# A sparse graph layer on one NeuronCore: the diagonal found among the candidates instead of in the full row, and the last tiles' order written anew

## The chip, the core and the metric

The kernel runs on one core of a Trainium2 chip. The metric is the time of the whole program on the device in microseconds, the median of several executions. Engines are named as in the profile: PE is TensorE, PEld its weight loads, DVE is VectorE, ACT is ScalarE, POOL is GpSimd, SP is SyncE, which only issues transfers.

## The reference

x is 8192x512 and adj is 8192x8192, both float32. adj is zero but for some nine entries a row (73,960 in all in the inputs that are drawn), the diagonal always among them, since it is `bernoulli(0.000488)` made symmetric, with the unit matrix added, times a uniform value between 0.05 and 5.42.

```python
h = max(layernorm(x), 0)
mask = adj > 0
head = mask / max(sqrt(sum(mask * mask, axis=-1)), 1e-12)
inc = adj + head
out = x + (inc @ h) / sum(inc, axis=-1)
```

So every row of the result is x plus a weighted mean of the few rows of h that its nonzero entries name.

## The kernel before

**Stages.** In the first 80 us the layer norm reads x, and h = relu(layernorm(x)) is written to a scratch tensor in DRAM. Then adj is read once, in 64 tiles of 128 rows. A tile is 128 x 8192 float32, 4 MB; it comes in four chunks of 1 MB, and a chunk j holds columns 1024j to 1024j+1023 of the left half and of the right half (runs of 4 KB). There are two tile buffers (`A`), so tile t+2 is loaded chunk by chunk into the buffer that tile t leaves (`load_chunk`, on SP's queue). A chunk may be overwritten when DVE has folded it and when ACT has run its two tests over the pair of chunks (`checked`).

**One tile on DVE.** For the first 61 tiles (`FOLDED`) DVE folds the two halves of a chunk into one word a column, right times 2^100 plus left (`fold`), takes the eight largest words (`find_values`) and their places (`find_places`). That is three passes of 1024 columns for each chunk, twelve a tile. Between them stand the small operations of the tile before, p = t-1, on 32 candidates a row (8 from each of 4 chunks): `tell_halves`, `low_words`, `values`, `counts` (which signs are set, and how many), `ranks` (the place of each spilled entry), `columns_any`, `columns`, `own_columns`, `heads`, `incs`, `inverse`, `weights`; and those of tiles t-2 and t-3 (`pay_places`; `find_entry`, `take_entry`, `sum_entry`). The two best candidates of every chunk are the row's own slots (8), the other 24 can spill: what is set among them is packed for the 128 rows together into 3 x 128 places by matmuls (`offsets`, `find_owner`, `bring_spill`). The last three tiles (61 to 63, "wide") are searched without folding, in eight parts of 1024 columns, and after them comes a batch tile (number 64, `BATCH`, here also called z) that does those rows again which the folded way could not do; its row numbers are found by `count_bad`, `pay_bad`, `pick_bad` and `list_rows` while the wide tiles run, and its adj rows come by one indirect transfer.

**The diagonal.** Of each folded tile the diagonal entry is treated apart. `read_diagonal` takes a strided 128x128 block of the chunk, multiplies it with the unit matrix and sums it to one value a row; `cut_diagonal` sets the diagonal's word in `F` to zero, so that it is no candidate; `keep_diagonal` copies the value to the front of the candidates. Its row of h is not gathered but computed again from x by ACT (`row_again`) and added by a matmul (in `residual`).

**The others.** POOL gathers rows of h from DRAM: 8 indirect transfers for the own slots (`gather_own`), 3 or 4 for the spilled ones (`gather_spill`); empty slots have a column beyond the tensor and are skipped. ACT builds the diagonal weight matrices (`own_matrices`), the spill matrix (`spill_matrix`), the root of the count (`roots`), the places (`reach_places`), and runs the tests (`check`, four a tile). PE multiplies: x by the unit matrix and the row again (`residual`), 8 own slots (`product_own`), 3 or 4 spill groups (`product_spill`). ACT copies the sum out (`finish_tile`), SP stores it.

**What sets the order.** Each engine's program is written out by hand: `period(t)` for tile t on ACT, DVE and PE, `wide_period` and `batch_period` on DVE, and `drain` for what is left when the last tile has been searched. Within `period(t)` p = t-1, q = t-2, r = t-3 and f = t-4. Nothing is scheduled otherwise. In the drains and in the batch period z, y, w and v are tiles 64, 63, 62 and 61.

## Time and profile before

| | |
|---|---|
| median of 3 runs | 1268.82 us (1267.47 to 1271.12) |
| the profiled execution, its own time | 1271.85 us |
| its span from first to last instruction | 1270.1 us |
| busy: PE, DVE, ACT, POOL | 78%, 94%, 77%, 60% |
| transfers | 471.00 MB, mean 371 GB/s |
| mean granted clock of TensorE | 0.905 |

The engines' shares say how busy each was over the span; the DMA share of a stretch is the mean over the core's 16 transfer engines. The span has three parts: the layer norm (to about 80 us), the loop over the folded tiles (to 1127 us), and the wide tiles with the batch tile and the drain (to 1270 us).

### The profile page before, as it was taken

To read this page: it belongs to the slowest core of one execution; us is meant where nothing else is said; L and a number is where in the kernel's file an instruction comes from. 1 tells how busy PE (TensorE), PEld (TensorE's weight loads), DVE (VectorE), ACT (ScalarE), POOL (GpSimd) and SP (SyncE) were. 2 spreads that over 40 slices of the span, in tenths; PEclk is the share of its full clock that TensorE was granted. 3 is DMA by queue.
4 is the path that set the end of the run, shared out by engine and by line. 5 is a ranking of instruction groups with operands and counts; after the bars stand their busy time and mean duration, and the time that the engine had idled before them with its cause. 6 is when DMAs were issued, how large, how long until landed. Compare 5 with 4: busy or idle time off the path is not lost.

```text
span 1270.1 us, 14707 instructions
## 1 busy us (share of the span) xinstructions
PE 987.8 (78%) x2682; PEld 483.4 (38%) x2682; DVE 1189.0 (94%) x2868; ACT 979.2 (77%) x1902; POOL 765.8 (60%) x748
## 2 busy tenths in 40 slices
PE   0003888988898899888889879888978898777677
PEld 0001444444444344444444334433433444443343
DVE  6679999999999999999999999999999999999971
ACT  6657788888888888888888888787887888884741
POOL 1003666666666676667666666667666677665562
PEclk9999899888889988888998998889888898888888
DMA  8999999999999999999999999999999999997542
GB/s 353 427 423 406 398 392 381 393 388 390 388 391 401 398 399 394 400 400 398 399 401 391 396 394 387 390 395 400 400 385 381 395 386 387 397 399 259 175 118 77
DMA packets 148208, 471.00 MB, mean 371 GB/s; under 512 B 24826, under 2 KB 24826, under 8 KB 143965
## 3 DMA queue, kind: packets, MB, share of 16 engines
q1 hardware_dynamic: 90368, 331.38, 66.4%
q0 software_dynamic: 57744, 138.64, 30.0%
q8 instruction: 25, 0.41, 0.1%
q14 instruction: 71, 0.58, 0.1%
HBM read 490.47 MB, written 33.82 MB: 413 GB/s over the span
## 4 chain that ended last, share of the span: by engine, by line
DVE 47%; DMA 25%; issue 14%; ACT 5%; SPq 4%; PE 4%; POOL 0%; DVEq 0%; another core or an unknown queue 0%; ACTq 0%; POOLq 0%
DMA adj_tile<-in_adj_dram 22%; DVE cand_word L797 14%; DVE folded L775 14%; DVE cand_index L801 5%; DMA gathered_rows<-in_x_dram 3%; DVE cand_index L820 2%; DVE cand_word L815 2%; PE acc L1330 2%; SPq L392 2%; ACT adj_tile L563 2%; ACT junk L576 1%; SPq L399 1%; PE acc L1341 1%; DVE diagonal_alone L782 1%; DVE entry L964 1%
## 5 line engine op out<-in xcount | busy, mean ns | idle before, releaser
L497 POOL DMA_INDIRECT gathered_rows<-h_scratch,slot_column x520 | 552.4, 1062 | 263.9 <-issue 158.6
L576 ACT ACTIVATE junk<-adj_tile,zero_unit 128x2048 bf16<-128x2048 f32 x256 | 510.4, 1997 | 89.8 <-issue 45.9
L1330 PE MATMUL acc<-gathered_rows,diag 128*128 128x512 f32 x1040 | 517.9, 655 | 2.4 <-DMA gathered_rows<-h_scratch,slot_column 1.9
L497 POOL DMA_INDIRECT gathered_rows<-h_scratch,spill_column x198 | 205.3, 1037 | 212.9 <-ACT spill_column L622 157.8
L1330 PEld LDWEIGHTS acc<-gathered_rows,diag 128*128 128x128 f32 x1040 | 216.9, 215 | 259.7 <-issue 258.9
L775 DVE SCALAR_TENSOR_TENSOR folded<-adj_tile 128x1024 f32<-128x1024 f32 x244 | 296.6, 1216 | 10.0 <-DMA adj_tile<-in_adj_dram 8.7
L797 DVE MAX8 cand_word<-folded 128x8 f32<-128x1024 f32 x244 | 298.7, 1224 | 3.6 <-issue 0.3
L801 DVE FIND_INDEX8 cand_index<-cand_word,folded 128x8 uint32<-128x1024 f32 x244 | 297.6, 1220 | 0.0
L1341 PE MATMUL acc<-gathered_rows,spill_matrix 128*128 128x512 f32 x396 | 182.4, 597 | 16.1 <-DMA gathered_rows<-h_scratch,spill_column 13.0
L639 ACT ACTIVATE diag<-ident,weights_and_payload 128x128 f32<-128x128 f32 x581 | 176.4, 388 | 21.9 <-DVE weights_and_payload L917 17.7
L1279 PE MATMUL poff<-spill_rank,lanes_before 128*128 128x1 f32 x130 | 24.1, 255 | 157.5 <-DVE spill_rank L862 156.3
L1341 PEld LDWEIGHTS acc<-gathered_rows,spill_matrix 128*128 128x128 f32 x396 | 72.0, 190 | 108.2 <-issue 108.1
L1324 PE MATMUL acc<-own_row,diag 128*128 128x512 f32 x122 | 76.7, 715 | 46.1 <-ACT own_row L649 20.4
L1279 PEld LDWEIGHTS poff<-spill_rank,lanes_before 128*128 128x128 f32 x130 | 24.9, 217 | 207.5 <-issue 123.0
L1302 PE MATMUL pbrought<-weights_and_payload,owner 128*128 128x72 f32 (+1 forms) x384 | 69.6, 328 | 17.2 <-DVE weights_and_payload L922 16.5
L1308 PE MATMUL pturned<-ident,owner 128*128 128x128 f32 x396 | 80.2, 356 | 2.2
L1308 PEld LDWEIGHTS pturned<-ident,owner 128*128 128x128 f32 x396 | 68.2, 253 | 6.6 <-ACT spill_matrix L630 6.0
L1319 PE MATMUL acc<-x_residual,ident 128*128 128x512 f32 x96 | 53.0, 636 | 19.9 <-issue 11.1
L1302 PEld LDWEIGHTS pbrought<-weights_and_payload,owner 128*128 128x128 f32 x384 | 60.4, 232 | 18.4 <-issue 18.3
L630 ACT ACTIVATE spill_matrix<-pturned,entry 128x128 f32<-128x128 f32 x198 | 56.8, 357 | 0.8 <-PE acc L1341 0.8
L1324 PEld LDWEIGHTS acc<-own_row,diag 128*128 128x128 f32 x122 | 21.4, 211 | 93.2 <-issue 58.8
L622 ACT ACTIVATE spill_column<-entry 128x3 uint32<-128x3 f32 (+1 forms) x65 | 13.0, 199 | 52.3 <-DVE entry L964 51.3
(151 smaller groups left out, 892.8 us busy)
## 6 DMA issues: line engine op xcount, KB each, us to landing
adj_tile<-in_adj_dram SPq DMA_DIRECT2D x256, 1024.0 KB
h_scratch<-adj_tile SPq DMA_DIRECT2D x16, 1024.0 KB, 10.5
out_dram<-out_tile SPq DMA_DIRECT2D x64, 256.0 KB
gathered_rows<-in_x_dram SPq DMA_DIRECT2D x12, 1024.0 KB, 12.6
x_residual<-in_x_dram SPq DMA_DIRECT2D x48, 256.0 KB
gathered_rows<-h_scratch,slot_column POOLq DMA_INDIRECT x520
x_held<-in_x_dram SPq DMA_DIRECT2D x4, 1024.0 KB, 7.9
gathered_rows<-h_scratch,spill_column POOLq DMA_INDIRECT x198, 3.5
```

The lines of the kernel that those rows point to most:

```text
L497: nc.gpsimd.indirect_dma_start(out=into, out_offset=None, in_=h[:, :], in_offset=bass.IndirectOffsetOnAxis(ap=column, axis=0), bounds_chec ...
L576: nc.scalar.activation(junk[:, n % 2].rearrange("p (j c) -> p j c", j=2), both[:, :, half], ACT.Relu, bias=zero_unit[:], scale=-UP, accum_ ...
L630: last = nc.scalar.activation(W[:, t % 2, g], pturned[:, g * P:(g + 1) * P], ACT.Copy, scale=entry[:, t % 2, g, 0:1])
L639: last = nc.scalar.activation(diag[:, t % 2, s], ident[:], ACT.Copy, scale=wpay[:, t % 2, s:s + 1])
L775: nc.vector.scalar_tensor_tensor(out=F[:, j % 2], in0=a[:, 1], scalar=UP, in1=a[:, 0], op0=ALU.mult, op1=ALU.add).then_inc(folded, 1)
L797: nc.vector.max(out=cv[:, t % 2, 8 * j:8 * j + 8], in_=F[:, j % 2]).then_inc(vals_found, 1)
L801: nc.vector.max_index(out=ci[:, t % 2, 8 * j:8 * j + 8], in_max=cv[:, t % 2, 8 * j:8 * j + 8], in_values=F[:, j % 2]).then_inc(idx_found, 1)
L1302: last = nc.tensor.matmul(bank[:, c:c + 3 * n], owner[:, g * P:(g + 1) * P], wpay[:, t % 2, 1 + OWN:1 + OWN + 3 * n], start=True, stop=True)
L1308: last = nc.tensor.matmul(pturned[:, g * P:(g + 1) * P], owner[:, g * P:(g + 1) * P], ident[:], start=True, stop=True)
L1324: nc.tensor.matmul(acc[t % 3][:], diag[:, t % 2, 0], again[:], start=False, stop=False)
L1330: last = nc.tensor.matmul(acc[t % 3][:], diag[:, t % 2, 1 + s], slot(t % 2, s), start=False, stop=False)
L1341: last = nc.tensor.matmul(acc[t % 3][:], W[:, t % 2, g], slot(t % 2, OWN + g), start=False, stop=(g == groups(t) - 1))
```

## The change

The loads stay as they are (runs of 4 KB). Three things change.

First, on DVE the three operations on the diagonal go (`read_diagonal`, `cut_diagonal`, `keep_diagonal`). The diagonal's word stays in `F` and so becomes a candidate like any other. After the search of tile p a new `find_diagonal(p)` compares the eight column numbers of the chunk that holds the diagonal with the row's own number (a new constant `diag_at`), multiplies with the eight values and sums them into the front of the candidates; `leave_diagonal(p)` subtracts what was found, so that the candidate counts as unset. `columns_any` comes earlier for this, `counts` and `ranks` later. The load no longer waits for `diag_read`. Three steps of `count_bad` on the diagonal go as well.

Second, on ACT `row_again(t)` waits for `row_added` (the matmul that read the row of tile t-1) instead of `own_done` (all own products of tile t-1), and `roots` comes behind `spill_matrix`.

Third, the orders of DVE, ACT, PE and POOL are written anew from tile 61 on.

```diff
             def fold(t, j):
...
-                if j == diag_chunk(t):
-                    read_diagonal(t)
-                    cut_diagonal(t)
...
+            def find_diagonal(t):
+                dve.wait_ge(cola_ready, t + 1)
+                dve.wait_ge(val_ready, t + 1)
+                nc.vector.scalar_tensor_tensor(out=own_entry[:], in0=in_diag_chunk(cola, t), scalar=diag_column(t),
+                                               in1=in_diag_chunk(val[:, 1:], t), op0=ALU.is_equal, op1=ALU.mult,
+                                               accum_out=val[:, 0:1]).then_inc(diag_found, 1)
+
+            def leave_diagonal(t):
+                dve.wait_ge(diag_found, t + 1)
+                rest = in_diag_chunk(val[:, 1:], t)
+                nc.vector.tensor_tensor(rest, rest, own_entry[:], ALU.subtract).then_inc(diag_left, 1)
...
             def row_again(t):
                 if t >= 1:
-                    act.wait_ge(own_done, t)
+                    act.wait_ge(row_added, t)
...
             # ACT, period(t)
                     if not wide(q):
                         row_again(q)
-                if small:
-                    roots(p)
                 if pay:
                     copy_owner(q)
...
                     spill_columns(r)
                     spill_matrix(r)
+                if small:
+                    roots(p)
...
             # DVE
             def wide_period(t):
                 p, q, r = t - 1, t - 2, t - 3
                 part_values(t, 0)
+                if p == FOLDED:
+                    no_diagonal()
+                pay_places(q)
                 tell_halves(p)
...
                 part_values(t, 4)
-                pay_places(q)
...
             def batch_period():
...
                 part_values(z, 0)
-                find_entry(v)
+                pay_places(w)
                 tell_halves(y)
                 low_words(y)
-                take_entry(v)
...
                 part_places(z, 3)
-                pay_places(w)
...
             # POOL
                 gather_spill(t - 2)
-                gather_own(t)
+                if t < BATCH:
+                    gather_own(t)
             gather_spill(BATCH - 1)
+            gather_own(BATCH)
             gather_spill(BATCH)
```

**DVE, one folded tile.** These rows of before are the start of the program of tile 34, from its first fold, where the diagonal lies in the first chunk (lines are those of the kernel before; L782 is `read_diagonal`, L791 `cut_diagonal`, L841 `keep_diagonal`, L855 `counts`):

```order
L775 SCALAR_TENSOR_TENSOR folded<-adj_tile 128x1024
L782 SCALAR_TENSOR_TENSOR diagonal_alone,diagonal_value<-adj_tile,ident 128x128
L791 TENSOR_TENSOR folded<-folded,zero_on_diagonal 128x128
L922 SCALAR_TENSOR_TENSOR weights_and_payload<-spill_rank,half_minus_offset,entry_sign 128x24
L826 TENSOR_SCALAR right_half,right_counts<-cand_word 128x32
L831 SCALAR_TENSOR_TENSOR left_word<-cand_word 128x32
L797 MAX cand_word<-folded 128x8
L836 SCALAR_TENSOR_TENSOR entry_value<-cand_word,left_word 128x32
L841 COPY entry_value<-diagonal_value 128x1
L944 TENSOR_TENSOR own_entry<-pbrought,place_plus_half 128x72
L801 MAX_INDEX cand_index<-cand_word,folded 128x8
L855 TENSOR_SCALAR entry_sign,counts<-entry_value 128x33
```

The same place after the change (L919 is `pay_places`, L865 `columns_any`, L827 `find_diagonal`, L951 `take_entry`):

```order
L774 SCALAR_TENSOR_TENSOR folded<-adj_tile 128x1024
L919 SCALAR_TENSOR_TENSOR weights_and_payload<-spill_rank,half_minus_offset,entry_sign 128x24
L808 TENSOR_SCALAR right_half,right_counts<-cand_word 128x32
L813 SCALAR_TENSOR_TENSOR left_word<-cand_word 128x32
L779 MAX cand_word<-folded 128x8
L818 SCALAR_TENSOR_TENSOR entry_value<-cand_word,left_word 128x32
L865 SCALAR_TENSOR_TENSOR column_if_any<-right_half,cand_index 128x32
L941 TENSOR_TENSOR own_entry<-pbrought,place_plus_half 128x72
L783 MAX_INDEX cand_index<-cand_word,folded 128x8
L827 SCALAR_TENSOR_TENSOR diagonal_entry,entry_value<-column_if_any,diagonal_column,entry_value 128x8
L951 TENSOR_TENSOR taken<-pbrought,own_entry 128x144
L774 SCALAR_TENSOR_TENSOR folded<-adj_tile 128x1024
```

The two blocks of 128x128 and the copy are gone, `columns_any` has come forward from behind the second fold, and `counts` no longer stands behind the first search. It stands further down now; these rows follow directly (L834 is `leave_diagonal`, L852 `counts`, L859 `ranks`, L872 `columns`, L881 `own_columns`):

```order
L834 TENSOR_TENSOR entry_value<-entry_value,diagonal_entry 128x8
L961 TENSOR_REDUCE entry<-taken 128x6
L779 MAX cand_word<-folded 128x8
L852 TENSOR_SCALAR entry_sign,counts<-entry_value 128x33
L783 MAX_INDEX cand_index<-cand_word,folded 128x8
L859 SCALAR_TENSOR_TENSOR spill_rank<-entry_sign 128x24
L872 SCALAR_TENSOR_TENSOR column_less_base<-entry_sign,column_if_any 128x32
L881 TENSOR_TENSOR slot_column<-column_less_base,slot_base 128x8
L888 TENSOR_TENSOR weights_and_payload<-minus_spill_base,column_less_base 128x24
```

`ranks` stood before the second MAX and now stands behind the second MAX_INDEX, and `own_columns` now follows `columns` with nothing between.

**PE, the last products.** These rows of before begin with the offsets of tile 63 in PE's period 64 (L1279 `offsets`, L1302 and L1308 `bring_spill`, L1330 `product_own`, L1287 `find_owner`, L1341 `product_spill`, L1319 the x part of `residual`; `acc2` is tile 62, `acc1` tile 61 and later z, `acc0` tile 63):

```order
L1279 MATMUL poff<-spill_rank,lanes_before 128x1
L1302 MATMUL pbrought<-weights_and_payload,owner 128x168 x2
L1302 MATMUL ptr<-weights_and_payload,owner 128x168 x2
L1308 MATMUL pturned<-ident,owner 128x128 x4
L1330 MATMUL acc2<-gathered_rows,diag 128x512 x8
L1287 MATMUL powner<-from_first_place,half_difference 128x512
L1341 MATMUL acc1<-gathered_rows,spill_matrix 128x512 x4
L1319 MATMUL acc0<-x_residual,ident 128x512
L1330 MATMUL acc0<-gathered_rows,diag 128x512 x4
L1302 MATMUL pbrought<-weights_and_payload,owner 128x168 x2
L1302 MATMUL ptr<-weights_and_payload,owner 128x168 x2
L1308 MATMUL pturned<-ident,owner 128x128 x4
```

After the change the same place, from x of tile 62 (L1331 is `product_own`, L1342 `product_spill`):

```order
L1319 MATMUL acc2<-x_residual,ident 128x512
L1302 MATMUL pbrought<-weights_and_payload,owner 128x168 x2
L1302 MATMUL ptr<-weights_and_payload,owner 128x168 x2
L1308 MATMUL pturned<-ident,owner 128x128 x4
L1331 MATMUL acc2<-gathered_rows,diag 128x512 x4
L1279 MATMUL poff<-spill_rank,lanes_before 128x1
L1331 MATMUL acc2<-gathered_rows,diag 128x512 x4
L1287 MATMUL powner<-from_first_place,half_difference 128x512
L1342 MATMUL acc1<-gathered_rows,spill_matrix 128x512 x4
L1302 MATMUL pbrought<-weights_and_payload,owner 128x168 x2
L1302 MATMUL ptr<-weights_and_payload,owner 128x168 x2
L1308 MATMUL pturned<-ident,owner 128x128 x4
```

The offsets of tile 63 have moved behind `bring_spill` of tile 62 and the first four own products, and `bring_spill` of tile 63 has moved ahead of its own products. The rest of the program before, down to the last product, is:

```order
L1279 MATMUL poff<-spill_rank,lanes_before 128x1
L1287 MATMUL powner<-from_first_place,half_difference 128x384
L1302 MATMUL pbrought<-weights_and_payload,owner 128x168 x3
L1308 MATMUL pturned<-ident,owner 128x128 x3
L1330 MATMUL acc0<-gathered_rows,diag 128x512 x4
L1341 MATMUL acc2<-gathered_rows,spill_matrix 128x512 x4
L1407 MATMUL poff<-batch_marks,ones 1x64
L1319 MATMUL acc1<-own_row,ident 128x512
L1330 MATMUL acc1<-gathered_rows,diag 128x512 x8
L1341 MATMUL acc0<-gathered_rows,spill_matrix 128x512 x4
L1341 MATMUL acc1<-gathered_rows,spill_matrix 128x512 x3
```

and after:

```order
L1319 MATMUL acc0<-x_residual,ident 128x512
L1331 MATMUL acc0<-gathered_rows,diag 128x512 x8
L1342 MATMUL acc2<-gathered_rows,spill_matrix 128x512 x4
L1279 MATMUL poff<-spill_rank,lanes_before 128x1
L1319 MATMUL acc1<-own_row,ident 128x512
L1287 MATMUL powner<-from_first_place,half_difference 128x384
L1302 MATMUL pbrought<-weights_and_payload,owner 128x168 x3
L1308 MATMUL pturned<-ident,owner 128x128 x3
L1342 MATMUL acc0<-gathered_rows,spill_matrix 128x512 x4
L1331 MATMUL acc1<-gathered_rows,diag 128x512 x8
L1418 MATMUL poff<-batch_marks,ones 1x64
L1342 MATMUL acc1<-gathered_rows,spill_matrix 128x512 x3
```

Tile 62's spill product now comes before the offsets of z, and tile 63's before z's own products; before they stood behind z's `bring_spill`, and behind z's own products. PE has the same products, in another order.

## Rows read from the trace of the kernel before

**Rows 1.** The page: busy time by engine; GB/s in 40 equal slices.

```profile
PE 987.8 (78%) x2682; PEld 483.4 (38%) x2682; DVE 1189.0 (94%) x2868; ACT 979.2 (77%) x1902; POOL 765.8 (60%) x748
GB/s 353 427 423 406 398 392 381 393 388 390 388 391 401 398 399 394 400 400 398 399 401 391 396 394 387 390 395 400 400 385 381 395 386 387 397 399 259 175 118 77
```

**Rows 2.** Stretches of the span: length, each engine's busy time, clock, DMA share, GB/s.

```profile
131.10:351.80 220.70, 195.62 (x532) 98.54 (x531) 219.81 (x522) 185.55 (x363) 142.99 (x143) 0.90 1.02 390
351.80:761.00 409.20, 361.84 (x986) 168.20 (x984) 406.71 (x961) 341.54 (x670) 275.10 (x265) 0.92 1.03 397
761.00:1110.50 349.50, 298.21 (x812) 147.44 (x813) 339.32 (x801) 283.76 (x560) 243.23 (x219) 0.88 1.02 391
```

**Rows 3.** The same stretches, DVE's folds (L775) alone; four folds are one tile.

```profile
131.10:351.80 220.70, 63.12 (x53) 0.90 1.02 390
351.80:761.00 409.20, 116.72 (x96) 0.92 1.03 397
761.00:1110.50 349.50, 97.28 (x80) 0.88 1.02 391
```

**Rows 4.** DVE in order of time, tile 34: start, duration, instruction.

```profile
660.07 0.38 DVE L782 SCALAR_TENSOR_TENSOR diagonal_alone<-adj_tile,ident 128x128 f32<-128x128 f32 x1
660.67 0.24 DVE L922 SCALAR_TENSOR_TENSOR weights_and_payload<-spill_rank,half_minus_offset,entry_sign 128x24 f32<-128x24 f32 x1
...
668.07 0.15 DVE L884 TENSOR_TENSOR slot_column<-column_less_base,slot_base 128x8 uint32<-128x8 f32 x1
668.14 0.18 DVE L891 TENSOR_TENSOR weights_and_payload<-minus_spill_base,column_less_base 128x24 f32<-128x24 f32 x1
668.23 1.22 DVE L775 SCALAR_TENSOR_TENSOR folded<-adj_tile 128x1024 f32<-128x1024 f32 x1
669.49 1.23 DVE L797 MAX8 cand_word<-folded 128x8 f32<-128x1024 f32 x1
...
673.14 0.25 DVE L900 SCALAR_TENSOR_TENSOR inc<-entry_value,head,entry_sign 128x33 f32<-128x33 f32 x1
673.32 1.22 DVE L797 MAX8 cand_word<-folded 128x8 f32<-128x1024 f32 x1
```

**Rows 5.** ACT's waits before its tests, 675 to 1110.5 us: total, times, longest.

```profile
ACT junk L576 <- issue: 40.5, 22, 3.9
ACT junk L576 <- DMA adj_tile<-in_adj_dram: 28.2, 19, 4.1
```

**Rows 6.** PE in order of time, tile 34's period and the drain; idle before in brackets.

```profile
665.55 0.38 PE L1279 MATMUL poff<-spill_rank,lanes_before 128*128 128x1 f32 x2 [1.81 <-DVE spill_rank L862]
...
667.89 8.34 PE L1330 MATMUL acc<-gathered_rows,diag 128*128 128x512 f32 x16
...
1210.38 1.46 PE L1302 MATMUL pbrought<-weights_and_payload,owner 128*128 128x168 f32 x4 [4.96 <-DVE weights_and_payload L922]
...
1236.15 2.05 PE L1302 MATMUL pbrought<-weights_and_payload,owner 128*128 128x168 f32 x6 [0.67 <-issue]
1237.99 1.49 PE L1308 MATMUL pturned<-ident,owner 128*128 128x128 f32 x6
...
1248.03 7.03 PE L1330 MATMUL acc<-gathered_rows,diag 128*128 128x512 f32 x16
1254.90 6.17 PE L1341 MATMUL acc<-gathered_rows,spill_matrix 128*128 128x512 f32 x14
```

**Rows 7.** POOL in order of time: first and last of ten gathers in a row.

```profile
1205.62 1.00 POOL L497 DMA_INDIRECT gathered_rows<-h_scratch,spill_column  x1 [0.30 <-issue]
...
1217.34 1.00 POOL L497 DMA_INDIRECT gathered_rows<-h_scratch,slot_column  x1 [0.30 <-issue]
```

**Rows 8.** DVE in order of time: first search of tile z, a sum_entry, last search.

```profile
1197.53 1.21 DVE L815 MAX8 cand_word<-adj_tile 128x8 f32<-128x1024 f32 x1
...
1217.50 0.62 DVE L964 TENSOR_REDUCE entry<-taken 128x8 f32<-128x448 f32 x1
...
1220.56 1.22 DVE L820 FIND_INDEX8 cand_index<-cand_word,adj_tile 128x8 uint32<-128x1024 f32 x1
```

## What the change will do, forecast before it ran

> **What bounds the kernel now.** I read the page first: DVE is busy for 94% of the span, PE for 78%, and the transfers run at 380 to 401 GB/s in every slice of the loop over the folded tiles [rows 1]. So there are two candidates, DVE and the transfers, and a share over the whole span cannot tell them apart.
>
> Next I cut the loop into stretches at the start of a tile's first fold [rows 2] and counted the folds in each [rows 3]. From 131.1 to 351.8 us there are 52 further folds, 13 tiles, in 220.7 us: 16.98 us a tile, with DVE idle for 0.9 us in all. From there to 761.0 us, 24 tiles take 17.05 us each, DVE idle for 2.5. The last 20 tiles take 17.475 us each, and DVE is idle for 10.2. So DVE is the bound of about two thirds of the loop, and of the last third it is not alone.
>
> The third view says what comes in. From 675 us on ACT waits before its tests 41 times, 68.7 us in total [rows 5]. The test has nothing to wait for but its chunk, so I read the part that is put down to "issue" as the same wait for transfers. The view of 351.8 to 592 us has no such line. That fits the rates: 17.475 us at 391 GB/s are 6.83 MB a tile. The first 16 tiles load no x, and need 16.98 times 390, 6.62 MB. At 401, the best slice of the gathering part of the loop [rows 1], 6.83 MB take 17.03 us. **From tile 17 on the transfers need 17.03 to 17.5 us a tile, and DVE needs 16.98: the kernel has two bounds within 3% of each other.**
>
> The end has a third one. The last search of the batch tile starts at 1220.56 us [rows 8], and the last product ends at 1254.90 + 6.17 = 1261.07 [rows 6]. What follows (copy, indirect store, its landing) is 9.0 us to the span's end at 1270.1. PE is late there because at 1210.38 it stood 4.96 us before `bring_spill` of tile 62, until DVE had done `pay_places(w)`, which was written far down in the batch period, and all products queue behind.
>
> **The change, DVE in the loop.** `read_diagonal` and `cut_diagonal` take from 660.07 to 660.67, 0.60 us a tile [rows 4]. The copy goes too. It is not costlier than the two small operations that take 0.16 together, from 668.07 to 668.23: 0.07. Removed are 0.67. `find_diagonal` is a scalar_tensor_tensor with a sum over 8 columns. I have no such row; from below it is a small operation (0.08), from above the same form over 33 columns, 673.14 to 673.32, 0.18. I take 0.15, since the reading of the sum is part of both. `leave_diagonal` is 0.08. `own_columns` now stands directly behind `columns`, from which it reads. An operation that need not wait starts 0.09 before the end of the one ahead (668.23 against 668.14 + 0.18), one that must starts 0.04 behind it (669.49 against 668.23 + 1.22). That is 0 to 0.13, I take 0.10. Added are 0.33, saved 0.34 a tile, 0.28 to 0.51 by the bounds: DVE's tile goes from 16.98 to 16.64 us. The Trainium skill (VectorE: DVE Perf Modes, The DRAIN you can't avoid) says that a semaphore between two Vector operations costs nothing extra; by that the saving would be 0.44, and the row with 0.13 between the two kinds of start disagrees.
>
> **What of it reaches the end.** In the first 15 tiles or so DVE is the only bound. 6.62 MB in 16.64 us are 398 GB/s, just under the best slice, so all is gained: 15 x 0.34 = 5.1 us. If only 394 GB/s were to be had there, 16.80 us a tile, it would be 2.7. In the 44 tiles from 351.8 to 1110.5 us (758.7 us at a mean of 394 GB/s) the bytes are the same, because a gathered row is a gathered row in either kind of slot. 16.64 us would want 410 GB/s, which no slice there has. At 401 throughout they would take 745.5, 13 less; at the late stretch's 391, reached sooner because the stock of loaded chunks is eaten sooner, 765, 6 more. ACT's tests release the buffers, and their order against the chunk's arrival hardly changes, so I see no reason for either end; with DVE less often late I take 1 us less. **The loop gives 6 us, between -4 and +18.**
>
> The waits that move in the loop cost nothing by my reading. `ranks` ends some 8.6 us after the tile's start instead of 6.5, and PE waited for it already: 1.81 us at 665.55 [rows 6]. PE comes to the offsets later too, since everything behind them (`bring_spill`, 8.3 us of own products) shifts along. PE's 15.05 us a tile (195.62/13) plus a wait of 1.2 fit in 16.64. The own products then end about 3 us into the next tile, behind the end of `own_matrices`, and here the finer wait earns its place: with `own_done` ACT would stand before `row_again`, with `row_added` it doesn't. `roots` late lets ACT go through `spill_matrix` while `counts` is still to come; the second test starts at about +7.6 us as before. POOL's 11 gathers at 1.30 (11.72/9, [rows 7]) are 14.3 us, under 16.64.
>
> Letting the diagonal be a candidate pushes others out of the own slots. Counted in the inputs, spilled entries go from 277 to 317 a tile on average; one tile has 389 for 384 places. Rows for the batch tile go from 51 to 60, and 128 fit. So no dense pass is started and no transfer is added.
>
> **The wide tiles and the end.** On DVE tile 61 gets longer by about 0.4 us (the diagonal of tile 60, and three more pairs of searches with nothing between, 0.13 each at most). Tile 62 loses three steps that each wait for the one ahead, some 0.25 each, net 0.5. Tile 63 takes over the three entry operations of tile 61, about 1.5 us (their last alone is 0.62 [rows 8]), and the batch period gives these away but gets those of tile 63. The last search ended at 1220.56 + 1.22 = 1221.8 and now ends 1.4 later, at 1223.2, before any gain of the loop.
>
> I walk PE from there with the durations of [rows 6]. `pay_places` of tiles 60 to 62 comes at the start of their period, so PE no longer stands before `bring_spill`, and is through with tile 61 when tile 63's gathers land. POOL issues them from about 1205 (its columns come 6 us into the batch period, which starts at 1197.5 + 1.4 [rows 8]): 8 x 1.30 to 1215.4. So PE starts on tile 63's own products at about 1218; 7.03 to 1225.1; spill product of 62, 6.17 x 8/14 = 3.5, to 1228.6. Now `finish_tile(62)` stands ahead of `roots(z)` on ACT, an estimated 0.6; root, places and weights of z 2.0 (ten small operations of some 0.2); with offsets, x and owner of z beside them, `bring_spill(z)` starts at 1231.2 and takes 2.05 + 1.49 to 1234.7. Spill product of 63, 3.5, to 1238.2; z's own products 7.03, to 1245.2; marks 0.2; z's 3 spill groups 6.17 x 6/14 = 2.6, to **1248.0 instead of 1261.1: 13 us**. POOL fits: z's own gathers from 1226.5 to 1237, its spill gathers behind `finish_tile(63)` on ACT, from 1239.7 to 1243.6, landed at 1245. From below the end gains 3 (two stalls like the 4.96 put somewhere else), from above 16 (ACT's two copies no longer felt).
>
> **Sum.** 6 + 13 = 19 us: the profiled execution's span would go from 1270.1 to 1251, its own time from 1271.85 to 1253. The runs' median, 1268.82, stands 3.0 under the profiled time, so I forecast 1250.
>
> **Rivals.**
> - *DVE is the bound throughout* (chance 0.13). Then 60 x 0.34 = 20.4, and 13 at the end: 1235. For it: DVE waits only 2.5 us up to 761. Against it: ACT's 41 waits, and 410 GB/s. The Trainium skill (DMA: Bandwidth & Descriptors, Specifications) gives the fabric a ceiling of 435 GB/s, by which 6.83 MB would take an estimated 15.7 us and this rival would hold; the layer norm's slices with up to 427 agree with the ceiling, the gathering slices stay at 401. The same table's 358 GB/s for a core's share of HBM is passed by every slice of the loop.
> - *The transfers get better only in part* (0.15): loop 9 to 15, end 13: 1241 to 1247.
> - *The end does not move* (0.13): the finish copies that now stand ahead of `roots(z)` and of z's spill columns cost what `pay_places` gave. Loop 6, end 3: 1260.
> - *Slower* (0.05): PE becomes the bound. 15.05 us a tile are at a granted clock of 0.90; at 0.83 they are 16.3, with the wait for the late `ranks` 17.5, against 17.18 on average now (979.4/57). 0.3 x 57 = 17, less 13: 1273. It decides from a clock of about 0.85 down. Against it: the stretches grant 0.88 to 0.92 with PE as busy as it will be.
>
> **How the numbers follow.** My forecast (1245 to 1256) has 0.50, and 0.04 is left for no change to speak of. A difference within 0.3% (1265.0 to 1272.6) is about what a measurement of this kernel cannot tell from none. Faster: 0.50 + 0.13 + 0.15 + 0.12 = 0.90; of the third rival's 0.13 one hundredth falls within 0.3%, so same is 0.04 + 0.01 = 0.05; slower 0.05. The range 1237 to 1262 leaves out the far half of the first rival, the slower one and the rest.
>
> **What would show it.** In the profile after: no 128x128 operation on DVE in the loop; folds 16.6 us a tile apart up to about 350 us (step 1), 17.1 to 17.5 later, and ACT's waits before its tests starting well before 675 us (step 2); PE's wait before the offsets of about 1 us (the late ranks are free); no wait before `row_again`; last product 13 us closer to the last search, less 1.4 (step 3). I am wrong if the folds stay 16.7 apart to the end, if ACT waits for `own_row` or `root`, or if PE stands in the drain.

## The result, and the profile after

The changed kernel took 1261.69 us (median of 4 runs, 1260.84 to 1262.61) against 1269.97 for the kernel before (4 runs, 1267.47 to 1271.48): a ratio of 0.994, 95% interval 0.9926 to 0.9955. It is 8.3 us faster where 19 were forecast. Measured again later on three chips, the same kernel gave 0.9992 (0.9979 to 1.0004), 0.9995 (0.9985 to 1.0005) and 0.9993 (0.9984 to 1.0003): there nothing is left of the gain that can be told from none. Both findings have to be explained.

The profiled execution took 1262.61 us, its span is 1260.9. From its page come the busy times and the GB/s in 40 slices [rows 1], and the groups of ACT's test and of PE's product with the own row:

```profile
PE 964.9 (77%) x2682; PEld 480.2 (38%) x2682; DVE 1170.5 (93%) x2801; ACT 976.3 (77%) x1902; POOL 774.1 (61%) x746
GB/s 362 426 424 406 398 399 393 394 393 392 398 386 401 400 399 391 396 399 395 380 398 388 393 394 386 393 391 383 397 393 374 377 384 392 392 397 345 172 187 92
L569 ACT ACTIVATE junk<-adj_tile,zero_unit 128x2048 bf16<-128x2048 f32 x256 | 510.5, 1995 | 149.5 <-DMA adj_tile<-in_adj_dram 149.3
L1324 PE MATMUL acc<-own_row,diag 128*128 128x512 f32 x122 | 79.4, 738 | 53.6 <-ACT own_row L642 53.4
```

DVE lost 18.5 us of work (1189.0 before), and ACT stands 149.5 us before its tests. PE stands 53.4 us before the product that adds the row which ACT computes again (L1324; 20.4 before, and 15.9 put down to "issue"). The stretches start at the first folds of tiles 3, 16 and 40 as before, all engines first [rows 2]:

```profile
130.33:347.40 217.07, 189.23 (x534) 96.13 (x533) 215.73 (x510) 185.79 (x363) 147.09 (x143) 0.91 1.02 395
347.40:758.20 410.80, 355.73 (x984) 175.82 (x983) 399.58 (x937) 337.94 (x671) 280.22 (x263) 0.90 1.03 394
758.20:1112.10 353.90, 296.42 (x821) 145.28 (x820) 333.49 (x781) 284.46 (x561) 243.20 (x221) 0.91 1.02 388
```

and then DVE's folds alone, 52, 96 and 80 of them (one more at the edge of the last) [rows 3]:

```profile
130.40:347.38 216.98, 63.26 (x52) 0.91 1.02 395
347.38:758.21 410.83, 116.79 (x96) 0.90 1.03 394
758.21:1112.14 353.93, 97.33 (x81) 0.91 1.02 388
```

A tile takes 16.69 us in the first stretch (16.98 before), 17.12 in the second (17.05 before) and 17.70 in the third (17.475 before). Tile 16 starts 4.4 us sooner, tile 40 is 2.8 sooner, tile 60 1.6 later (1112.1 against 1110.5). **The loop gave its gain back.** ACT's waits before its tests, from 675 us to the fold of tile 60, are 85.0 us where they were 68.7 [rows 5]. Before, 40.5 of these were put down to "issue"; here all are put down to the chunk, so that reading of "issue" was right:

```profile
ACT junk L569 <- DMA adj_tile<-in_adj_dram: 85.0, 47, 3.8
```

PE in order of time in the end, and DVE's two waits for its products (in brackets: idle before) [rows 6, 8]:

```profile
1208.58 0.73 PE L1302 MATMUL ptr<-weights_and_payload,owner 128*128 128x168 f32 x4
...
1223.67 7.03 PE L1331 MATMUL acc<-gathered_rows,diag 128*128 128x512 f32 x16
1230.54 3.60 PE L1342 MATMUL acc<-gathered_rows,spill_matrix 128*128 128x512 f32 x8
...
1236.80 1.12 PE L1302 MATMUL pbrought<-weights_and_payload,owner 128*128 128x168 f32 x6 [0.67 <-ACT owner L607]
...
1249.03 2.84 PE L1342 MATMUL acc<-gathered_rows,spill_matrix 128*128 128x512 f32 x6
```

```profile
1209.35 0.27 DVE L941 TENSOR_TENSOR own_entry<-pbrought,place_plus_half 128x112 f32<-128x112 f32 x1 [0.23 <-PE ptr L1302]
...
1222.12 0.28 DVE L941 TENSOR_TENSOR own_entry<-pbrought,place_plus_half 128x112 f32<-128x112 f32 x1 [2.22 <-PE ptr L1302]
```

No 4.96 us before `bring_spill` any more. PE's products close up from 1207 us on, with 0.59 and 0.67 us idle, and the last ends at 1251.87 instead of 1261.07. Of this 9.2 us the walk through the end gave 10.8 (1251.87 - 1112.14 = 139.7, before 1261.07 - 1110.55 = 150.5), and the loop took 1.6.

### The profile page after: what moved, and what is told of

Read it like the earlier page. It is cut to its first block, busy times and chain, and to the rows that moved or that the text cites. A ratio compares the mean times of both kernels' runs of the same rounds, so it can differ in the third digit from the quotient of the medians.

```text
span 1260.9 us, 14638 instructions
## 1 busy us (share of the span) xinstructions
PE 964.9 (77%) x2682; PEld 480.2 (38%) x2682; DVE 1170.5 (93%) x2801; ACT 976.3 (77%) x1902; POOL 774.1 (61%) x746
## 4 chain that ended last, share of the span: by engine, by line
DMA 56%; DVE 22%; issue 11%; ACT 5%; PE 3%; SPq 2%; POOL 0%; ACTq 0%; DVEq 0%; POOLq 0%
DMA adj_tile<-in_adj_dram 47%; DVE folded L774 7%; DVE cand_word L779 5%; DMA x_residual<-in_x_dram 5%; DMA gathered_rows<-in_x_dram 3%; DVE cand_index L783 2%; PE acc L1331 2%; ACT adj_tile L556 2%; DVE cand_word L797 1%; ACT junk L569 1%; PE acc L1342 1%; DVE cand_index L802 1%; DMA gathered_rows<-h_scratch,spill_column 1%; SPq L385 1%; ACT diag L632 1%
## 5 line engine op out<-in xcount | busy, mean ns | idle before, releaser
L488 POOL DMA_INDIRECT gathered_rows<-h_scratch,slot_column x520 | 546.4, 1051 | 263.6 <-issue 157.6
L569 ACT ACTIVATE junk<-adj_tile,zero_unit 128x2048 bf16<-128x2048 f32 x256 | 510.5, 1995 | 149.5 <-DMA adj_tile<-in_adj_dram 149.3
L1331 PE MATMUL acc<-gathered_rows,diag 128*128 128x512 f32 x1040 | 495.5, 632 | 0.9 <-DMA gathered_rows<-h_scratch,slot_column 0.8
L488 POOL DMA_INDIRECT gathered_rows<-h_scratch,spill_column x198 | 220.1, 1112 | 200.3 <-ACT spill_column L615 157.4
L1331 PEld LDWEIGHTS acc<-gathered_rows,diag 128*128 128x128 f32 x1040 | 209.7, 208 | 242.9 <-issue 242.9
L1342 PE MATMUL acc<-gathered_rows,spill_matrix 128*128 128x512 f32 x396 | 187.2, 610 | 25.7 <-DMA gathered_rows<-h_scratch,spill_column 25.7
L1279 PE MATMUL poff<-spill_rank,lanes_before 128*128 128x1 f32 x130 | 24.8, 260 | 161.1 <-DVE spill_rank L859 161.1
L1324 PE MATMUL acc<-own_row,diag 128*128 128x512 f32 x122 | 79.4, 738 | 53.6 <-ACT own_row L642 53.4
L1342 PEld LDWEIGHTS acc<-gathered_rows,spill_matrix 128*128 128x128 f32 x396 | 73.7, 194 | 119.0 <-issue 118.8
L1279 PEld LDWEIGHTS poff<-spill_rank,lanes_before 128*128 128x128 f32 x130 | 28.3, 237 | 209.7 <-issue 130.2
L1319 PE MATMUL acc<-x_residual,ident 128*128 128x512 f32 x96 | 54.8, 654 | 33.8 <-DMA x_residual<-in_x_dram 33.6
L1308 PE MATMUL pturned<-ident,owner 128*128 128x128 f32 x396 | 77.1, 347 | 0.0
L1302 PE MATMUL pbrought<-weights_and_payload,owner 128*128 128x72 f32 (+1 forms) x384 | 71.2, 334 | 1.6 <-ACT owner L607 1.6
L1308 PEld LDWEIGHTS pturned<-ident,owner 128*128 128x128 f32 x396 | 67.2, 250 | 0.0
L1302 PEld LDWEIGHTS pbrought<-weights_and_payload,owner 128*128 128x128 f32 x384 | 62.8, 240 | 2.9 <-ACT owner L607 1.9
L1324 PEld LDWEIGHTS acc<-own_row,diag 128*128 128x128 f32 x122 | 23.5, 219 | 97.3 <-ACT diag L632 83.2
L649 ACT ACTIVATE out_tile<-acc 128x512 f32<-128x512 f32 x65 | 37.6, 578 | 19.1 <-PE acc L1342 19.1
## 6 DMA issues: line engine op xcount, KB each, us to landing
h_scratch<-adj_tile SPq DMA_DIRECT2D x16, 1024.0 KB, 10.8
```

The costliest lines, as they stand in the source:

```text
L488: nc.gpsimd.indirect_dma_start(out=into, out_offset=None, in_=h[:, :], in_offset=bass.IndirectOffsetOnAxis(ap=column, axis=0), bounds_chec ...
L569: nc.scalar.activation(junk[:, n % 2].rearrange("p (j c) -> p j c", j=2), both[:, :, half], ACT.Relu, bias=zero_unit[:], scale=-UP, accum_ ...
L1302: last = nc.tensor.matmul(bank[:, c:c + 3 * n], owner[:, g * P:(g + 1) * P], wpay[:, t % 2, 1 + OWN:1 + OWN + 3 * n], start=True, stop=True)
L1308: last = nc.tensor.matmul(pturned[:, g * P:(g + 1) * P], owner[:, g * P:(g + 1) * P], ident[:], start=True, stop=True)
L1324: nc.tensor.matmul(acc[t % 3][:], diag[:, t % 2, 0], again[:], start=False, stop=False).then_inc(row_added, 1)
L1331: last = nc.tensor.matmul(acc[t % 3][:], diag[:, t % 2, 1 + s], slot(t % 2, s), start=False, stop=False)
```

## The experiments

**Padding, release and bytes: who sets the late tiles?** Four edits of the changed kernel. e1_pad:

```diff
+                if j == diag_chunk(t):
+                    nc.vector.scalar_tensor_tensor(out=picked[:], in0=tri[:], scalar=1.0, in1=ident[:], ...)
+                    nc.vector.tensor_tensor(cut[:], tri[:], ident[:], ALU.min)
```

> The changed kernel with two 128x128 DVE operations put back behind the fold of the diagonal's chunk; they read two constants and write tiles that nobody reads, so DVE's tile is 17.0 us again and all else is as in the changed kernel (1261.7 us). Theory T (after the first 20 tiles the transfers set the loop, and the 0.34 us a tile are only used to eat the stock of loaded chunks sooner): the time stays at 1258 to 1265, the fold of tile 61 starts within 2 us of 1128.9, DVE's waits for chunks nearly go. Rival D (DVE's shorter tile is what gained, and something else lost it again at the end): 0.3 x 60 = 18 us slower, about 1280. If the gain of 6.8 us at tile 23 counts at all, about 1268.

e2_early, in ACT's period:

```diff
                 check(t, 0)
+                if t < FOLDED:
+                    check(t, 1)
...
-                check(t, 1)
+                if t >= FOLDED:
+                    check(t, 1)
```

> The changed kernel with ACT's second test of a tile directly behind its first (tiles 0 to 60), so that the first pair of chunks is given back some 5 us sooner and its reload is issued sooner. Theory A (the loop over release, load and test is what holds the late tiles at 17.45 us: the buffer is held too long, and the queues run short of loads): tiles 20 to 60 take 17.1 to 17.2 us, 8 to 14 us less in all, about 1250. Theory B (391 GB/s is what this mix of transfers gives, whenever the loads are issued): the loads only take longer from issue to landing, and the time stays within 3 us of 1261.7. Rival to both: own_matrices and row_again come 2 us later behind a test that now waits for its chunk, PE comes late, and it is slower by up to 5 us.

e3_late, in `load_chunk`:

```diff
-                    sp.wait_ge(checked, 4 * (t - 2) + 2 * (j // 2) + 2)
+                    sp.wait_ge(checked, 4 * (t - 2) + 3 + j // 2)
```

> The changed kernel with the loads of a tile's first pair of chunks waiting for the third test of the tile two before instead of its second, some 2 to 3 us later. Theory A (time from release to landing counts): the late tiles get up to 1 us longer, 1275 to 1300. Theory B (only the rate counts): within 4 us of 1261.7, the median time from issue to landing falls by about the delay.

e4_nox loads no x for tiles 16 to 60:

```diff
-            return held[:, t] if t < HELD else xres[:, t % 2]
+            return held[:, t % HELD] if t < FOLDED else xres[:, t % 2]
...
-                if t >= HELD:
+                if t >= FOLDED:
                     load_x(t)
```

> The changed kernel without the loads of x for tiles 16 to 60: held rows of other tiles are used in their place, so 45 x 256 KB = 11.8 MB are not moved and the output is not the reference's. A tile then moves 6.57 MB instead of 6.83. Theory B (bytes): 0.26 MB at 391 GB/s are 0.67 us a tile, but DVE's 16.69 us are the next bound, so the late tiles take 16.7 to 16.85 us and the end comes 25 to 30 us sooner, 1232 to 1237. Theory A (issue too late): the bytes matter less, some 5 to 10 us, 1252 to 1257.

Measured on one chip, beside 1274.49 us for the kernel before: e1_pad 1275.48 (ratio 1.0007, 0.9986 to 1.0028), e2_early 1275.71 (1.0014, 0.9989 to 1.0039), e3_late 1275.59 (1.0018, 0.9994 to 1.0042), e4_nox 1261.32 (0.9881, 0.9846 to 0.9916). All are some 10 us and more over what theories T and B gave them; e1_pad stands near its rival's 1280 and e3_late at the lower end of theory A's 1275 to 1300, so by the times alone they would speak against T and B. But one and the same thing lies in all four traces: DVE stands 12.0 to 12.3 us before the entries of tile 62, and in the loop now and then up to 4.3 us where it waits for PE, for ACT or for its own result. The first trace of the changed kernel has nothing of the kind, so these four can't be weighed against its 1261.7. Next to them belong the changed kernel itself, e2 beside it, and two edits that undo a part of the change, all four on one other chip.

> The changed kernel once more, unchanged, beside the kernel before. Its first measurement gave a ratio of 0.994. In the traces of the four kernels before this one, ACT and DVE both stand some 12 us in the batch period behind products of PE that had long been recorded as issued, and in the loop DVE stands up to 5 us behind its own results; the trace of the changed kernel had neither. If that comes with the place and the time of the run, this run shows it too, about 10 us later than 1261.7 while the fold of tile 61 stays near 1129; if it comes with the edits, this run is at 1261.7 again.

> The second test directly behind the first, a second time, beside the changed kernel on the same chip. The first trace had tiles 37 to 50 at 16.7 us with no wait for a chunk, against 17.3 in the changed kernel, but also 25 us of other waits on DVE, in which the transfers could catch up. Theory A (release too late): without such waits the late tiles take 17.1 to 17.2 and it is 5 to 12 us faster than the changed kernel. Theory B (rate): within 3 us of it.

e5_paylate, DVE's batch period, in the order of the kernel before for places and entries (`pay_places(y)` comes later too, and `find_entry(y)` stands in the drain):

```diff
-                pay_places(w)
...
                 part_places(z, 3)
+                pay_places(w)
...
+                pay_places(y)
+                find_entry(w)
```

> The changed kernel with DVE's order in the batch period put back for the places and the entries: pay_places(w) behind the fourth search, find_entry(w) behind pay_places(y), find_entry(y) behind the searches. The theory that early places are what the end gained: PE stands some 5 us before bring_spill(w) again and everything behind it moves, 5 to 9 us slower than the changed kernel. Rival: what gained is the order of PE's products and ACT's copies, and PE has the slack in the batch period: within 2 us of the changed kernel.

e6_owndone, in `row_again`:

```diff
-                    act.wait_ge(row_added, t)
+                    act.wait_ge(own_done, t)
```

> The changed kernel with ACT's own row waiting for the last own product of the tile before (own_done), as before the change. Theory of the prediction: own products end about 3 us into the next tile, so ACT now stands before row_again for up to 3 us a tile, its second test and so the release of the first pair of chunks come that much later, and the time grows by 0 to 10 us. Rival: ACT waits for chunks anyway from tile 20 on, and the wait is hidden: within 2 us.

Beside 1272.76 us for the kernel before: c_after 1271.77 (0.9992, 0.9979 to 1.0004), e2b_early 1272.84 (1.0006, 0.9993 to 1.0019), e5_paylate 1272.72 (1.0005, 0.9991 to 1.0019), e6_owndone 1271.53 (0.9993, 0.998 to 1.0006). The long wait is the chip's and not the edits': c_after, in every line the changed kernel, has it. Rows of PE, DVE and ACT of c_after in order of time:

```profile
1208.67 0.73 PE L1302 MATMUL ptr<-weights_and_payload,owner 128*128 128x168 f32 x4
1209.24 1.05 PE L1308 MATMUL pturned<-ident,owner 128*128 128x128 f32 x8
1210.13 3.60 PE L1331 MATMUL acc<-gathered_rows,diag 128*128 128x512 f32 x8
1213.56 0.28 PE L1279 MATMUL poff<-spill_rank,lanes_before 128*128 128x1 f32 x2
1213.70 3.68 PE L1331 MATMUL acc<-gathered_rows,diag 128*128 128x512 f32 x8
1220.86 0.38 PE L1287 MATMUL powner<-from_first_place,half_difference 128*128 128x512 bf16 x1 [3.48 <-ACT from_first_place L600]
```

```profile
1219.58 0.27 DVE L941 TENSOR_TENSOR own_entry<-pbrought,place_plus_half 128x112 f32<-128x112 f32 x1 [11.90 <-remote]
```

```profile
1209.71 0.28 ACT L585 ACTIVATE root<-counts,count_eps 128x1 f32<-128x1 f32 x1
1219.78 0.17 ACT L593 ACTIVATE half_minus_offset<-poff 128x1 f32<-128x1 f32 x1 [9.79 <-remote]
```

The reader is to see that two engines start within 0.2 us of each other, one on a product of PE that ended at 1209.4 by its rows, the other on one that ended at 1213.8, while PE itself went on. Not the products are late but their signals, that is, the updates of semaphores by which an engine tells the others that a product is done. In the loop the fold of tile 60 comes at 1110.2 us as against 1112.1: the loop is the same. All of the 10 us is in the end, from that fold to the end of the last product: 150.6 us against 139.7.

As for the theories: e2b_early and c_after have equal times and tile 60 at 1111.2 and 1110.2 us, so an earlier release brings nothing (theory A falls), and e3's later one costs no more than its other waits: tile 60 at 1114.2, with 12.5 us of DVE waits for late signals against 5.7 in c_after. The chips differ (e3 beside e1_pad's 1113.2 on one, c_after on another), so a cost of some 3 us of the later release (1114.2 against e2_early's 1111.1) is not ruled out; the up to 1 us a tile of theory A is. e6's `own_done` costs nothing (ACT waits before its own row 5 times, 6.5 us, beside some 124 us of waits before its tests). e5 costs nothing that can be told from noise either, where 5 to 9 us were forecast: PE stands 7.88 us before `bring_spill(w)` there, but DVE's 11.9 are gone.

**Are the signals held up by the gathers?** e7_nogather:

```diff
             def gather_own(t):
...
+                if t == BATCH - 1:
+                    return
...
             def product_own(t, g):
...
-                pe.wait_ge(own_gathered[t % 2][g], 16 * CHUNKS * turn(t))
+                if t != BATCH - 1:
+                    pe.wait_ge(own_gathered[t % 2][g], 16 * CHUNKS * turn(t))
```

> The changed kernel without the eight gathers of tile 63's own rows (its own products use the rows of tile 61, so the output is not the reference's). They run from 1207 to 1219 us, just while PE's signals are out, and in five traces the signals came 0.2 to 2.7 us after the last of them was issued. Theory G (the gathers hold the signals up): find_entry of tile 62 starts within 1 us of PE's row, and the end comes 8 to 10 us sooner than in the changed kernel on this chip. Rival S (it comes from PE's burst of 16 small products or from how the run is recorded): DVE stands some 10 us as before.

e10_order rewrites the batch period (of its edit these are PE's part and one of DVE's; ACT's and the drain are as the expectation says):

```diff
                 residual(w)
+                offsets(y)
                 bring_spill(w)
                 product_own(w, 0)
-                offsets(y)
+                find_owner(y)
                 product_own(w, 1)
-                find_owner(y)
...
-                find_entry(w)
                 part_places(z, 2)
...
                 part_values(z, 5)
+                find_entry(w)
```

> The changed kernel with a batch period that stands late signals of PE: offsets of tile 63 ahead of bring_spill of tile 62, its owner between the two halves of tile 62's own products, ACT's copy of that owner and the nine diagonals ahead of tile 62's spill matrix, and DVE's entry operations of tile 62 three searches later, those of tile 63 in the drain. Where the signals come 10 us late (1271.8 us): DVE searches on instead of standing 12 us, PE need not stand 5.6 us before tile 60's spill product, 5 to 9 us faster than the changed kernel. Where they come in time: within 2 us. Rival: the entries of tiles 62 and 63 are now late for POOL's spill gathers, and PE stands in the drain instead: no gain.

> The kernel before, one look. In the eight traces since the first of the changed kernel, PE's signals in the batch period come up to 12 us after its products' rows. In the trace of the kernel before, the signal of the batch tile's bring_spill came 6 us after its rows. Expected: 1270 to 1276 us, its loop as in the first trace (fold of tile 60 at 1110 to 1113), and the same late signal.

> The changed kernel as the control of this call: ratio to the kernel before 0.999 if the signals are late here too (DVE's wait at tile 62's entry near 12 us), 0.994 if they are not.

Beside 1272.17 us for the kernel before: c_before 1270.38 (one run), c_after2 1271.87 (0.9995, 0.9985 to 1.0005), e7_nogather 1263.48 (one run), e10_order 1268.46 (0.9968, 0.9958 to 0.9978). Without tile 63's gathers DVE's wait (11.2 us in c_after2) is this:

```profile
1208.98 0.28 DVE L943 TENSOR_TENSOR own_entry<-pbrought,place_plus_half 128x112 f32<-128x112 f32 x1 [1.60 <-PE ptr L1304]
...
1221.75 0.27 DVE L943 TENSOR_TENSOR own_entry<-pbrought,place_plus_half 128x112 f32<-128x112 f32 x1 [2.22 <-issue]
```

and the whole is 8.4 us shorter, within 2 us of the first measurement. The time isn't won by PE's own wait for the gathers, which the edit drops too: in c_after2 PE comes to these products at 1229.02 us and finds them landed. So theory G holds for this place, on the word of one run: with POOL's eight gathers away, PE's signals come in time there, and PE's burst of 16 small products alone doesn't make them late. Elsewhere in the same trace, in the loop, they are still up to 14 us late. Why they come in time on another chip with the gathers too is not shown. e10_order gained 3.4 us over c_after2, where 5 to 9 were forecast. The kernel before suffers as well, but elsewhere, and this stood in the trace that the prediction was read from. In c_before:

```profile
1234.94 2.05 PE L1302 MATMUL pbrought<-weights_and_payload,owner 128*128 128x168 f32 x6 [0.67 <-issue]
...
1243.62 0.33 DVE L944 TENSOR_TENSOR own_entry<-pbrought,place_plus_half 128x168 f32<-128x168 f32 x1 [7.48 <-remote]
```

The batch tile's entry starts 6.6 us after its product's end, while POOL still gathers. Its end takes no longer than the changed one's: from tile 60's fold to the start of the last single product 148.4 us (1258.7 - 1110.3), in c_after2 149.2.

**The pair with and without x.** The same padding, with the bytes there and away; and e12_order2, which is e10_order and, on PE, tile 63's first own products ahead of `bring_spill(y)`:

```diff
                 product_spill(v)
-                bring_spill(y)
                 residual(y)
                 product_own(y, 0)
+                bring_spill(y)
```

> The changed kernel without the loads of x for tiles 16 to 60, a second time, as the partner of the next run (the output is not the reference's). Theory of two bounds: with 6.57 MB a tile DVE's 16.68 us are the only bound; tiles 24 to 60 take 16.7 us each but for DVE's waits for late signals. Time as before, 1257 to 1262, ratio near 0.988.

> The same without the loads of x, and with the two idle 128x128 operations put back on DVE (17.06 us a tile). Theory of two bounds: now nothing hides DVE's 0.36 us, so tiles 16 to 60 get 44 x 0.36 = 16 us longer than in the run before, and the whole 19 to 22 us; with x loaded the same two operations cost 3 us up to tile 60. If DVE's tile does not matter even here, within 4 us of the run before.

> The kernel with the rewritten batch period (ratio 0.9968), and on PE x and the first half of tile 63's own products ahead of bring_spill of tile 63. PE stood 1.67 us there for DVE's taken and 1.45 for ACT's spill matrix; both lie beside products now: 3 us faster, ratio 0.9945. Rival: POOL's spill gathers of tile 63 and the own gathers of the batch tile move back by as much, and PE waits for them at its end: no gain.

These three came on a chip where the signals were in time. There e4b_nox is at the 1232 to 1237 us first put down for e4_nox. With late signals e4_nox took 28.4 us more: 19.0 of them up to the fold of tile 60 (1100.9 against 1082.0), for without x DVE waits for no chunk and every late signal is paid for in full, and 9.6 in the end. The 0.988 expected the second time was that of e4_nox. Beside 1269.16 us for the kernel before: e4b_nox 1232.92 (0.971, 0.9685 to 0.9735), e11_noxpad 1254.4 (0.9879, 0.9854 to 0.9903), e12_order2 1263.38 (0.9958, 0.9943 to 0.9972). The last three runs stood side by side on one more chip, with late signals:

> The changed kernel as the control of this call. With signals in time (DVE's wait at tile 62's entry under 2 us) a ratio of 0.994 to the kernel before; with late signals (11 to 12 us there) 0.999.

> The changed kernel with the two idle 128x128 operations, the cell that is missing beside the pair without x: there the padding cost 21.5 us. Theory of two bounds: with x the transfers bound the late tiles, so the padding costs only what the first 20 tiles gain and the chunk waits do not take back: fold of tile 60 0 to 4 us later than in the control, the time 0 to 5 us over it. If bytes and DVE simply add up, 20 us over it.

> The kernel with the twice rewritten batch period beside the control on one chip. With signals in time: 0.0 to 2 us slower than the control, since PE's products close up in both and tile 62's entries come later. With late signals: 6 us faster than the control.

Beside 1273.88 us: c_after3 1272.87 (0.9993, 0.9984 to 1.0003), e1b_pad 1277.41 (1.0018, 1.0007 to 1.003), e12b_order2 1270.32 (0.9983, 0.9965 to 1.0001). e1b_pad is 4.5 us over its control, inside the 0 to 5 expected, but its tile 60 comes 5.9 us later and not 0 to 4; e12b_order2 is 2.6 us faster than the control, where 6 were expected. The stretch from the fold of tile 20 to that of tile 60 is 40 tiles; here is the all-engine row of each kernel (third pair: DVE). The changed kernel, first trace, and c_after3, which ran beside e1b_pad:

```profile
414.12:1112.14 698.02, 594.60 (x1644) 291.65 (x1643) 666.80 (x1562) 565.66 (x1119) 477.95 (x439) 0.90 1.02 391
413.88:1110.60 696.72, 590.33 (x1641) 291.87 (x1640) 666.01 (x1561) 569.87 (x1119) 468.77 (x439) 0.91 1.02 391
```

e1b_pad, with x and padding:

```profile
422.36:1116.53 694.17, 590.67 (x1638) 292.53 (x1636) 680.09 (x1681) 569.94 (x1118) 470.42 (x441) 0.90 1.02 393
```

e4b_nox, without x:

```profile
413.78:1081.98 668.20, 582.33 (x1637) 295.00 (x1636) 663.55 (x1562) 573.37 (x1122) 458.43 (x441) 0.91 1.02 393
```

e11_noxpad, without x and with padding:

```profile
421.64:1104.26 682.62, 587.92 (x1642) 292.68 (x1640) 678.92 (x1681) 572.32 (x1120) 462.56 (x441) 0.90 1.01 385
```

In us a tile: with x 17.42 unpadded (17.45 in the first trace) and 17.35 padded; without x 16.71 and 17.07. **With x, 14.1 us more DVE work in this stretch cost nothing; without x, 15.4 us more cost 14.4.** Late signals could blur the pair with x, since both its traces have them, and c_after3 more. But all nine traces whose loop is the changed kernel's take 694 to 698 us for the stretch, those with signals in time too: what DVE doesn't lose to late signals it waits for chunks. In e4b_nox and e11_noxpad it waits for no chunk at all.

Over the whole program the padding cost 21.5 us without x (1254.4 - 1232.9) and 4.5 with it (1277.4 - 1272.9, both on the late-signal chip). Taking x away brought 28.8 us (1261.7 - 1232.9) where the signals were in time, and only 10 to 14 where they were late (e4_nox's 1261.3 beside c_after's 1271.8 on another chip; by their ratios, 0.9881 and 0.9992, it is 14). The rows also show the rate: 391 and 393 GB/s with x, 393 and 385 without it. That is two bounds side by side, as the prediction had it. The second one binds from tile 24 on in the changed kernel, where DVE waits for a chunk for the first time; in e1b_pad tiles 3 to 42 take DVE's 16.97 to 17.15 us, and it first waits for a chunk in tile 43.

The traces side by side, in us, with the last two columns the fold of tile 60 and the time from there to the end of the last product:

| trace | signals | fold of tile 20 | of tile 60 | the end |
|---|---|---|---|---|
| before, c_before | late | 420.1, 419.8 | 1110.6, 1110.3 | 150.5, 149.0 |
| changed, first trace | in time | 414.1 | 1112.1 | 139.7 |
| c_after, c_after2, c_after3 | late | 413.7 to 414.0 | 1109.6 to 1110.6 | 149.8 to 151.1 |
| e7_nogather | late, but in time at tile 62's entries | 413.8 | 1109.9 | 142.7 |
| e4b_nox, e11_noxpad | in time | 413.8, 421.6 | 1082.0, 1104.3 | 140.0, 140.6 |
| e12_order2 | in time | 413.8 | 1108.7 | 145.6 |
| e10_order, e12b_order2 | late | 413.8, 413.6 | 1110.5, 1108.0 | 148.7, 149.4 |
| e1b_pad | late | 422.4 | 1116.5 | 149.2 |

e4b_nox and e11_noxpad have the changed kernel's end, so on their chip too it takes 140 us. e12_order2, on the same chip, takes 5 us longer; among other things PE stands 2.12 us before the batch tile's own products, whose gathers now come later, as its rival said.

## Why the prediction was right and wrong

Of the 19 us forecast the first trace gave 9.2: the loop fell 7.6 short of its 6, the end 2.2 short of its 13.

**DVE's tile: right.** 16.69 us against 16.64. In the trace the search for the diagonal starts at 659.61 us and the next row at 659.75, 0.14 us where I took 0.15, with nothing lost behind it. The saving is 0.29 us (16.98 - 16.69), forecast 0.34. The Trainium skill (VectorE: DVE Perf Modes, The DRAIN you can't avoid) says, of eight copies in a row, that a semaphore between Vector operations costs nothing extra; the estimate by it is 0.44. The trace stands with the row of 0.13, and a little beyond it.

**"The loop gives 6 us": wrong, it gave none.** In the nine traces with the changed kernel's loop tile 60 comes at 1108.0 to 1112.1 us, 1109.8 in the mean; in the two of the kernel before at 1110.3 and 1110.6. The -1.6 of the first trace lies inside this scatter. The gain was there for a while: 4.4 us at tile 16, 6.0 at tile 20 (414.1 against 420.1), 6.7 at tile 23 (464.5 against 471.3). The failed step is what came behind it. The sentence "so all is gained: 15 x 0.34 = 5.1 us" carried this gain to the end, and the 44 tiles behind it were taken at their old 758.7 us, less 1. They took 764.8 (1112.1 - 347.4). That is the 765, "6 more", which I had worked out for the case that the stock of loaded chunks is eaten sooner, and saw no reason for.

The gain was a loan from this stock. Once tiles wait for chunks, the start of tile 60 is all bytes up to there over their mean rate, and it doesn't matter how soon the first tiles were folded. The rows say so: 131 to 1110.5 us at 390, 397 and 391 GB/s before is a mean of 393.3, and 395, 394 and 388 after is 392.1. The faster DVE only had the waits begin sooner: its first wait for a chunk is at 491.1 us, in tile 24, where before it was at 805.6, in tile 42. I had named both bounds, seen that the late bytes need 17.03 to 17.5 us a tile, and then added a gain of the one bound to a time of the other. The bound of -4 to +18 us did hold the -1.6. Where DVE is slower than the bytes the loan isn't called in: e1b_pad is 8.5 us behind its control at tile 20 and still 5.9 at tile 60.

**The end, 13 us: right in its mechanism where the signals are in time, 10.8 there; wrong by nearly all of it elsewhere**, where the end takes 149.8 to 151.1 us against 149.0 and 150.5 before. In the first trace two terms were mis-sized. Tile 61 took 22.6 us where my sum made it 21.3 (20.9 and 0.4): of that DVE stood 1.07 us for its root. Tile 63's own products began at 1223.67 us where 1218 was forecast; from there on the walk holds, 25.4 us to the last product's start against my 27.4 (1245.4 - 1218), for `bring_spill(z)` cost 1.12 + 0.83 and not 2.05 + 1.49. The same products ran at a granted clock of 1.00 there (the upper level, 2.4 GHz), behind 0.59 and 0.67 us of idle time, and at 0.50 before (the lower, 1.2 GHz), behind 3.80 and 0.67. I had taken these two durations from rows at the lower clock. `finish_tile(62)` ahead of `roots(z)` did make DVE wait, 4.39 us, but PE's products lay beside it. What the steps lacked altogether is the way of a signal from PE to DVE and ACT. On four of the five chips that ran experiments it was up to 12 us late in the batch period. There the early `pay_places` lets PE through sooner, and DVE, which now asks for tile 62's entries three searches sooner, stands 10 to 12 us for them; in the order of before it asked 2.3 us behind the product (1215.30 against 1212.96) and the answer had come. e5 shows the trade: 7.88 us before PE or 11.9 before DVE, and no difference in the time.

**The waits that move: nearly free, as said, but not as said.** PE's wait before the offsets was to be about 1 us; it is 2.1 a tile in the first stretch (27.8 us, 13 times), 1.7 before (22.3, 13 times), and there PE has the room. `row_added` was to spare ACT a wait; with `own_done` it is 6.5 us in the whole loop and the time the same (e6).

**The rivals.** "DVE is the bound throughout" is out by e1b_pad. "The transfers get better only in part" is out as well, since the loop gained nothing. "Slower, PE becomes the bound" too: the stretches grant a clock of 0.90 to 0.91, and PE is busy for 14.9 us of a tile's 17.45 (594.60/40). "The end does not move" came true on the chips with late signals, by another mechanism than the finish copies that I had named.

**A better version.** e10_order, with orders that don't ask for PE's answer so soon, is at 0.9968 where the changed kernel is at 0.9995, on one chip and without overlap of the intervals: 3.4 us. e12, one step further, is at 0.9983 beside 0.9993 on such a chip, and their intervals overlap; with signals in time its 0.9958 (0.9943 to 0.9972) is no better than the changed kernel's 0.994 (0.9926 to 0.9955), and its end is 5 us longer than that of e4b and e11 on the same chip. So e10 is worth having where signals are late; where they are not, the changed kernel's own order beats e12's, and e10 was not measured. The way to a faster loop is not in DVE but in the bytes: e4b's 11.8 MB less brought 28.8 us. There the shorter tile on DVE pays: padded back to 17.07 us a tile, the same kernel takes 1254.4 instead of 1232.9 (e11).

**Open** are three things. The first is how large the ratio is on one chip with signals in time: the trace of the kernel before that went with 0.994 has late ones, and the whole changed kernel was not measured on such a chip again. Its end was, in e4b and e11; with e12's 1263.38 us less the 5.3 that its end is longer, my estimate is 1258 us there, 0.991 of the 1269.16 for the kernel before. The second is why signals are late. The recording itself is a suspect, for the traces with late signals are the ones in which many events are missing (below), and no run here tells the two apart. The third is why the rate where tiles wait for chunks (388 to 394 GB/s) stays under the 397 of a stretch where DVE paced it [rows 2]; neither an earlier nor a later release moved it (389 to 391).

## What to carry to other kernels

When two engines' bounds lie within a few per cent, don't add a gain under the one to a time set by the other: what is gained before the second bound binds is a loan from its stock, unless that bound's own rate rises. To see which binds, pad the one and thin out the other, and read all four cells on the same stretch. And where a wait is taken away from one engine at a fixed stage, look at who now asks sooner for its answer, and repeat the measurement on another chip before a gain under 1% is believed.

## What the runs showed of the hardware

PE's signals can reach the other engines long after its products. In the first trace of the changed kernel, and in e4b, e11 and e12, all 520 updates of semaphores by PE's products are recorded, and each lies within 0.02 us of the end of its row. In the sixteen other traces 316 to 383 of PE's events are recorded (342 and 316 in the two of the kernel before, whose products make 459 updates), and in the loop some lie 1 to 15 us behind; those over 12 us are all of `bring_spill`, with its small products. The events of DVE and ACT are missing there too: 1041 to 1281 of DVE's against some 2294 in the four, and 491 to 616 of ACT's against some 959. Whether the missing records and the late signals have one cause is not shown.

In the loop this costs single waits: in c_after tile 28 took 20.3 us instead of 16.7, with 3.57 of it before the entries that PE brings. DVE's own signals are at times late too, so that it waits up to 3.0 us for its own last result (2.10 us before `leave_diagonal` in c_after). The kernel before took 1269.97 us in the first measurement and 1269.16 beside e4b, and 1272.2 to 1274.5 on the chips with late signals. A wait that the profile puts down to "remote" or "issue", on two engines at once and ended together, is the mark of it.

PE's small products cost nearly twice as much behind a pause: the six of `bring_spill(z)` took 2.05 us at a granted clock of 0.50, behind 3.80 and 0.67 us of idle time, and 1.12 at 1.00, behind 0.59 and 0.67.
